# A mixer's head: the order of convolution taps on VectorE, and of halo parts and scalings on GpSimd

## What is computed

```python
x = x + attn_a(layernorm(x))
x = x + ffn(layernorm(x))
x = x + attn_b(layernorm(x))      # the mixer: the change is here
x = x + ffn(layernorm(x))
```

```python
zxbcdt = x @ in_proj_w.T
z, xBC, dt = split(zxbcdt)                       # 512, 640 (x 512, B 64, C 64), 4 columns
dt = softplus(dt + dt_bias)
xBC = silu(causal_depthwise_conv(xBC, conv_w, width=4) + conv_b)
xs, B, C = split(xBC)                            # xs: 4 heads of 128
A = -exp(A_log)
y = ssd(xs * dt, A * dt, B, C) + xs * D          # chunked scan with a state per head
g = y * silu(z)
g = g * rsqrt(mean(g * g) + 1e-5) * norm_w
return g @ out_proj_w.T
```

## Time and profile before

| | us |
|---|---|
| median of 3 runs (546.05, 546.32, 546.50) | 546.32 |
| the profiled execution | 543.31 |
| its span, first to last instruction | 541.5 |
| busy in the span: PE / DVE / ACT / POOL | 517.0 / 402.6 / 310.8 / 127.1 |
| mixer's head, 329.5 to 363.0 | 33.5 |
| chunk loop and projections of the mixer, from 363.0 to about 418 | 55 |

### The profile page before, as it was taken

How to read it: one execution, slowest core, us unless ns; L and a number is a source line. 1 busy time by engine, 2 the same in 40 slices (tenths; PEclk the granted TensorE clock), 3 DMA queues, 4 the chain that set the end, 5 groups by cost and what they waited for, 6 DMA issues and landing times. The chain is left out here.

```text
span 541.5 us, 9132 instructions
## 1 busy us (share of the span) xinstructions
PE 517.0 (95%) x3035; PEld 436.8 (81%) x3037; DVE 402.6 (74%) x899; ACT 310.8 (57%) x768; POOL 127.1 (23%) x272
## 2 busy tenths in 40 slices
PE   5999999999999989999999999999898999999996
PEld 4778899998998977788887888757777778888885
DVE  5625565566566898799987899966886877898767
ACT  3656878588687643573443455889662254443342
POOL 2232424244243310000000004569533100000000
PEclk9999999999999999999999999999999999999999
DMA  7320100000002204000040000000000000000101
GB/s 273 116 79 1 40 2 2 2 0 2 2 2 70 83 1 142 1 1 1 0 137 0 2 1 0 2 0 2 0 1 2 0 1 1 1 1 0 40 1 39
DMA packets 5790, 14.25 MB, mean 26 GB/s; under 512 B 624, under 2 KB 2928, under 8 KB 5744
## 3 DMA queue, kind: packets, MB, share of 16 engines
q1 hardware_dynamic: 5744, 13.66, 7.3%
HBM read 12.61 MB, written 1.05 MB: 25 GB/s over the span
## 5 line engine op out<-in xcount | busy, mean ns | idle before, releaser
L170 PE MATMUL psum<-xT_hl,ffn_w_hl 128*128 128x512 f32 x312 | 77.7, 395 | 0.6 <-DVE f_t L1243 0.4
L170 PE MATMUL psum<-f_um,ffn_w_hl 128*128 128x512 f32 x288 | 72.2, 398 | 1.3 <-DVE f_t L1243 1.3
L170 PEld LDWEIGHTS psum<-xT_hl,ffn_w_hl 128*128 128x128 f32 x312 | 56.2, 188 | 12.2 <-issue 0.9
L170 PEld LDWEIGHTS psum<-f_um,ffn_w_hl 128*128 128x128 f32 x288 | 53.3, 188 | 14.2 <-DVE f_um L1255 2.1
L1140 ACT ACTIVATE f_sil<-psum 128x512 f32<-128x512 f32 (+1 forms) x48 | 28.6, 596 | 60.3 <-PE psum L170 60.0
L170 PE MATMUL psum<-wo_hl,oT_hl 128*128 128x256 f32 x384 | 50.8, 281 | 4.2 <-DVE oT_hl L705 2.6
L699 DVE TENSOR_TENSOR pT_hl<-psum,pT_hl 126x360 fp32r<-126x360 f32 (+1 forms) x44 | 23.6, 537 | 41.4 <-ACT pT_hl L606 41.4
L170 PEld LDWEIGHTS psum<-wo_hl,oT_hl 128*128 128x128 f32 x384 | 47.9, 188 | 7.1 <-DVE oT_hl L705 5.1
L170 PE MATMUL psum<-xT_hl,wq_hl 128*128 128x512 f32 x192 | 52.1, 407 | 0.6 <-ACT qT L572 0.6
L1243 DVE TENSOR_TENSOR f_t<-psum,f_sil 128x512 f32<-128x512 f32 (+1 forms) x48 | 33.2, 691 | 26.2 <-ACT f_sil L1140 25.4
L572 ACT ACTIVATE qT<-psum 128x512 f32<-128x512 f32 x32 | 35.0, 1094 | 29.0 <-PE psum L170 29.0
(11 more groups left out here) (242 smaller groups left out, 1121.4 us busy)
## 6 DMA issues: line engine op xcount, KB each, us to landing
w_raw<-in_wq SPq DMA_DIRECT2D x4, 512.0 KB, 3.3
w_raw<-in_wo SPq DMA_DIRECT2D x4, 512.0 KB, 3.3
ffn_w_raw<-in_ffn SPq DMA_DIRECT2D x3, 576.0 KB, 5.6
ffn_w_raw_far<-in_ffn SPq DMA_DIRECT2D x3, 576.0 KB, 5.2
ssd_w_raw<-in_ssd SPq DMA_DIRECT2D x3, 512.0 KB, 5.7
x_resid<-in_x SPq DMA_DIRECT2D x2, 512.0 KB, 4.4
out_x<-x_resid SPq DMA_DIRECT2D x4, 256.0 KB, 2.2
w_raw<-in_wk SPq DMA_DIRECT2D x1, 512.0 KB, 6.3
```

Of the source, the lines that this page charges most:

```text
L170: i = e.matmul(dst, lhs(a), rhs(b), start=start and n == 0, stop=stop and n == len(TERMS) - 1, **kw)
```

## The change

Nothing that is computed changes; the same 30 taps, 5 joins, silus and scalings are done, in another order.

- Taps: the order is written out as `CV_ORDER`, a list of (i, tap), and with few exceptions neighbouring instructions belong to different tiles. The small instructions of the layer norm, of dt and of the cumulative sum stand at other places between them; ahead of the cumulative sum are now 20 taps, before 18.
- Halo parts: GpSimd works them out for block 0 at once when its tile is there, and for the four heads together, in five instructions with a broadcast of the tap weights, when the last of them (i = 4) is there. Ten instructions in place of 25.
- GpSimd: after make_xd(1) come join(2), join(3), join(4), and behind them make_xd(2) and make_xd(3).
- ScalarE: last_tap(15) moves ahead from behind silu_z(18) to behind silu(3); silu(5) and silu(6) move between the last silu_z's. DA's exponential moves behind the first two exponentials of the loop.
- TensorE: a wait for tile i = 4's taps stands ahead of the cumulative sum's matmuls, since the bank is shared and that tile's last tap is now behind the reciprocal of the dt chain; the keep_busy batches are 4, 7 and 6 long, not 9, 8, 8 and 6.

```diff
-            CONV_RUNS = ((0,), (1,), (2, 3), (4,), (5,), (6, 7), (8, 9))
+            CV_ORDER = [(0, 1), (0, 2), (0, 3), (1, 1), (1, 2), (1, 3), (2, 1), (3, 1), (2, 2), (3, 2), (2, 3), (3, 3),
+                        (4, 1), (4, 2), (5, 1), (4, 3), (5, 2), (6, 1), (5, 3), (6, 2), (7, 1), (6, 3), (7, 2), (8, 1),
+                        (7, 3), (8, 2), (9, 1), (8, 3), (9, 2), (9, 3)]
...
+            def conv_done(e, i):
+
+                e.wait_ge(S["cv"], cv_at(i, TAPS))
...
                 e.wait_ge(S["dt_pool"], DT_DONE)
+                conv_done(e, 4)
                 e.matmul(bank(0)[:, 0:P], a_rep, upto, start=True, stop=True)
...
                     if c == 0:
                         e.wait_ge(S["ipz"], len(others))
-                        keep_busy(9, 6)
-                        e.wait_ge(S["cv"], cv_count(NC))
-                        keep_busy(8, 6)
+                        conv_done(e, NC - 1)
+                        keep_busy(4, 6)
                         e.wait_ge(S["sl"], NC)
-                        keep_busy(8, 6)
+                        keep_busy(7, 6)
                         e.wait_ge(S["L"], 1)
                         keep_busy(6, 6)
...
                 silu_z(16)
                 silu(3)
+                last_tap(15)
                 silu_z(17)
                 silu(4)
+                silu(5)
                 silu_z(18)
-                last_tap(15)
+                silu(6)
                 silu_z(19)
-                for i in range(NC // 2, NC):
+                for i in range(7, NC):
                     silu(i)
-                e.wait_ge(S["cm"], 3)
-                e.activation(DA, DA, ACT.Exp).then_inc(S["da"], 1)
...
                         e.activation(bank(1), bank(1), ACT.Exp).then_inc(S["L"], 1)
+                        if c == 0:
+                            e.wait_ge(S["cm"], 3)
+                            e.activation(DA, DA, ACT.Exp).then_inc(S["da"], 1)
...
-                conv(0)
+                conv((0, 1), (0, 2))
                 ln["norm"](e, 1)
-                conv(1)
+                conv((0, 3), (1, 1), (1, 2))
                 ln["lo"](e, 1)
-                conv(2, 3)
+                conv((1, 3), (2, 1), (3, 1), (2, 2), (3, 2), (2, 3), (3, 3))
...
-                conv(4)
+                conv((4, 1), (4, 2), (5, 1))
                 e.wait_ge(S["dt_pool"], 5)
                 e.reciprocal(R1, N1).then_inc(S["dt_dve"], 1)
-                conv(5)
+                conv((4, 3), (5, 2), (6, 1), (5, 3), (6, 2))
...
-                conv(6, 7)
-                conv(8, 9)
+                conv((7, 1), (6, 3), (7, 2), (8, 1), (7, 3), (8, 2), (9, 1), (8, 3), (9, 2), (9, 3))
...
+                def carries(n, tiles, last):
+
+                    e.wait_ge(S["tap"], last + 1)
+                    b0, nb = tiles.start, tiles.stop - tiles.start
+                    taps = par[:, PR_CW + CONV * b0:PR_CW + CONV * (b0 + nb)].rearrange("p (b k) -> p b k", b=nb)
+                    tap = lambda k, wide: taps[:, :, k:k + 1].broadcast_to([P, nb, wide])
+                    e.tensor_tensor(carry[:, tiles, :], halo[:, tiles, :], tap(0, TAPS), ALU.mult)
+                    e.tensor_tensor(parts[:, tiles, 0:2], halo[:, tiles, 1:3], tap(1, 2), ALU.mult)
+                    e.tensor_tensor(parts[:, tiles, 2:3], halo[:, tiles, 2:3], tap(2, 1), ALU.mult).then_inc(S["part"], 1)
...
+                carries(0, slice(0, 1), 0)
+                carries(1, slice(2, CB), NC // 2 - 1)
...
                 join(1)
-                for i in range(1, NH):
-                    make_xd(i)
-                    join(i + 1)
+                make_xd(1)
+                for i in range(2, NH + 1):
+                    join(i)
+                make_xd(2)
+                make_xd(3)
```

More of the change, by code:

```diff
@@ L1470, in mixer @@
             dst = lambda b: cb_pre[:, :] if b == 0 else xs[:, b - 2, :]
-            names = ("xda dtw dtv cs cm rhs mb sel gs da raw wh wl bcz ip tap ipz part carry join cv sl xd dt dt_dve dt_pool dt_act de L G xt X xdd wt ce Y St st1 st y g ghi glo g2 ss "
+            names = ("xda dtw dtv cs cm rhs mb sel gs da raw wh wl bcz ip tap ipz part join cv sl xd dt dt_dve dt_pool dt_act de L G xt X xdd wt ce Y St st1 st y g ghi glo g2 ss "
                      "ve ri O fin bt").split()
@@ L1489, in mixer @@
             NC = len(convs)
-            CONV_RUNS = ((0,), (1,), (2, 3), (4,), (5,), (6, 7), (8, 9))
+            CV_ORDER = [(0, 1), (0, 2), (0, 3), (1, 1), (1, 2), (1, 3), (2, 1), (3, 1), (2, 2), (3, 2), (2, 3), (3, 3),
+                        (4, 1), (4, 2), (5, 1), (4, 3), (5, 2), (6, 1), (5, 3), (6, 2), (7, 1), (6, 3), (7, 2), (8, 1),
+                        (7, 3), (8, 2), (9, 1), (8, 3), (9, 2), (9, 3)]
+            assert len(CV_ORDER) == TAPS * NC
             def cv_at(i, tap):
[L1495 to L1502, removed]
+                return CV_ORDER.index((i, tap)) + 1
+            def conv_done(e, i):
+                e.wait_ge(S["cv"], cv_at(i, TAPS))
             def bank_taken(e, n):
                 if n in convs:
-                    e.wait_ge(S["cv"], cv_count(convs.index(n) + 1))
+                    conv_done(e, convs.index(n))
                 else:
@@ L1641, in decays @@
                         e.wait_ge(S["cm"], 3)
[L1642 removed]
+                        conv_done(e, 5)
                     else:
@@ L1752, in silu @@
                     b, h = order[convs[i]]
-                    e.wait_ge(S["cv"], cv_count(i + 1))
+                    conv_done(e, i)
                     if h:
@@ L1846, in dve, with conv @@
                 ln["veps"](e, 1)
[L1848 to L1860, removed]
-                conv(0)
+                emitted = iter(CV_ORDER)
+                def conv(*taps):
+                    for i, d in taps:
+                        assert next(emitted) == (i, d)
+                        b, h = order[convs[i]]
+                        src = bank(IN_BANK[convs[i]])
+                        out = dst(b)[:, half(h)]
+                        tap = par[:, PR_CW + CONV * b + CONV - 1 - d:PR_CW + CONV * b + CONV - d]
+                        e.wait_ge(S["tap"], i + 1)
+                        if d > 1:
+                            e.wait_ge(S["cv"], cv_at(i, d - 1))
+                        e.scalar_tensor_tensor(out=out[:, d:HALF], in0=src[:, 0:HALF - d], scalar=tap,
+                                               in1=out[:, d:HALF], op0=ALU.mult, op1=ALU.add).then_inc(S["cv"], 1)
+                conv((0, 1), (0, 2))
                 ln["norm"](e, 1)
-                conv(1)
+                conv((0, 3), (1, 1), (1, 2))
                 ln["lo"](e, 1)
-                conv(2, 3)
+                conv((1, 3), (2, 1), (3, 1), (2, 2), (3, 2), (2, 3), (3, 3))
                 e.wait_ge(S["dt"], 1)
@@ L1984, in join @@
                     out = dst(b)[:, HALF:HALF + TAPS]
-                    e.wait_ge(S["cv"], cv_count(NC // 2 + i + 1))
-                    e.wait_ge(S["carry"], i + 1)
+                    conv_done(e, NC // 2 + i)
+                    e.wait_ge(S["part"], 3 if b == 0 else 6)
                     e.tensor_tensor(out, out, carry[:, b, :], ALU.add).then_inc(S["join"], 1)
```

18 lines of the change are left out of this document (7 added, 11 removed).

## The result

The changed kernel takes 541.55 us (median of 7 runs, 540.86 to 541.93). The kernel before, run beside it, now has a median of 544.15 us over 7 runs: the three of 546.05 to 546.5 that the prediction saw, and four new ones at 543.54 to 544.15. The ratio of the two is 0.9937, with a 95% interval of 0.9916 to 0.9958. The medians are 2.6 us apart, the forecast was 2.5. The profiled execution is at 540.87 us with a span of 539.1; by the same subtraction from the profiled execution of before the prediction had 540.8.

The account below looks back on a forecast made before the run. The head was taken as bound by whichever of VectorE's taps, GpSimd's order and ScalarE's queue releases silu(9) last. Taps 1.3, GpSimd's order 1.1 and DA's exponential 0.14 make 2.5 us: 546.32 becomes 543.8 us, range 542.6 to 546.0.

Parts of the forecast that it names:

- What bounds the head: Mixer's head: the loop's first exponential waits for silu(9), that for join(4), which GpSimd does only after make_xd(3).
- Alternating taps, 0.8 us: VectorE: a dependent neighbouring tap costs 0.20 us; four such neighbours instead of eight save 0.8 us.
- both idle times, 0.54: VectorE: its waits for the cumulative sum, 0.33 us, and for tile 15's first tap, 0.21 us, both go.
- the second wait: VectorE waiting for tile 15's first tap on ScalarE at 355.33 us, put at 0.21 us, to disappear.
- GpSimd's order, 1.1 us: GpSimd: with joins ahead of make_xd(2) and (3), join(4) waits only for the last tap; 1.1 us gained.
- ScalarE's queue: ScalarE must be through with silu(8) by 358.5 us; expected free at 358.5, with 359.6 as upper bound.
- DA's exponential, 0.14: ScalarE: moving this exponential from ahead of the loop to behind its first two exponentials gains 0.14 us.
- Halo parts, select(1), x_dt_decay under cover: GpSimd: halo work for tiles 1 to 4 and later select(1) cost nothing; x_dt_decay keeps 0.85 us of cover.
- The price of a fall there, 5.2 us: TensorE ahead of the loop: its clock falls, two chunks at half rate cost 5.2 us, giving 549.0; chance 0.06.
- Sum, 2.5 us: Whole head: 1.3 from taps, 1.1 from GpSimd's order and 0.14 from DA's exponential make 2.5 us; chance 0.67.
- 543.31 becomes 540.8; the median becomes 543.8: Whole kernel: 2.5 us taken off the profiled execution and off the three runs' median of 546.32 us.
- The rivals: Gaps not from dependence 0.05, alternation fails 0.05, no change 0.07, TensorE's clock falls 0.06, partial gain 0.10.

Follow-up runs that it names:

- a_taps_in_runs: The changed kernel with the taps in the old order (tiles 0, 1, 4, 5 alone, the others in pairs); median 543.66 us.
- best_order: The changed kernel with three more dependent neighbours taken apart in the tap order; median 540.76 us, ratio to the kernel before 0.9937.
- a_joins_between: The changed kernel with GpSimd's old order, make_xd and join alternating; median 544.68 us.
- a_busy_0: The changed kernel without any of the 17 keep_busy matmuls ahead of the loop, the waits kept; median 544.63 us.

## Why the prediction was right in its mechanism and wrong in its time

- **What bounds the head: right.** silu(9) was released by join(4), join(4) by make_xd(3). With the joins ahead, join(4) and silu(9) behind it wait for the last tap.
- **Alternating taps, 0.8 us, and both idle times, 0.54: right.** 1.3 foretold; from the first tap the last one ends 26.02 - 24.53 = 1.49 us earlier. The forecast counted 0.8 + 0.54 = 1.34. Of the 0.15 beyond that, 0.09 is the second wait, which cost 0.30 us and not the 0.21 that its row shows (a_taps_in_runs); 0.06 I can't name. best_order confirms the price of 0.20 for one more dependence. From the Trainium skill's "VectorE: DVE Perf Modes", section "The DRAIN you can't avoid", the prediction drew that a tap behind its own predecessor steps like any other; that is not borne out for these shapes, 0.86 against 0.655 in both records. The same section also says that an instruction that is not held starts earlier, which agrees with independent taps of 0.74 us that start 0.655 apart.
- **GpSimd's order, 1.1 us: right,** 1.04 by itself. The three terms do add in the whole change, 1.49 + 1.04 + 0.14 = 2.67. They don't when one is missing, since silu(9) starts with the last queue to arrive: without this order the rest is worth 0.53 (a_joins_between).
- **ScalarE's queue: right.** It was through with silu(8) at 358.31 (358.5 foretold), 0.27 us ahead of join(4).
- **DA's exponential, 0.14: right.**
- **Halo parts, select(1), x_dt_decay under cover: right,** x_dt_decay kept 1.02 us (0.85 foretold).
- **TensorE.** The gap was 1.29 us, 1.0 foretold; the clock held at 1.00. Not said: the shorter batches are needed for 1.07 us of the gain. The price of a fall there, 5.2 us, was three times too high: a_busy_0 paid 1.67 for it.
- **Sum, 2.5 us: right,** 2.67 at decays(1), 2.65 between the kernels with the filled gap, 2.6 between the medians.
- **"543.31 becomes 540.8; the median becomes 543.8": this is the step that failed.** The first half was measured at 540.87. The second half took the median of three runs for a property of the kernel. I had written that it lay 3.0 us above the profiled execution and did not ask why: a change of head can't be told from a level that an execution has by chance. All three runs lay where before's slowest lie, 545.5 to 546.5. The record of such an execution shows a slow start of 1.3 us and a fall of the clock behind the gap ahead of project(7) of 1.5 us, together more than the whole change. That those three runs had the lower clock is inferred from their times, since they have no record; two later executions at 546.1 do show it.
- **The rivals.** None took place: the alternation works, the loop does start on silu(9), the clock holds at 357 to 372 us. The fall that I had looked for in the head sat 55 us later, in the kernel before as well.

## What to carry to other kernels

When several queues meet at one instruction, it starts with the last of them, and an edit shows its worth only once the others are out of the way: two parts of this change worth 1.04 and 0.53 us alone gave 2.55 together, and matmuls without use that were counted for the old wait took back 1.07 of it when kept. Where a profiled execution and the timed runs stand further apart than the change is worth, find out first what the difference is, by the granted clock beside each run, and forecast a difference or work from the execution that you have read. A gap of 1 us on TensorE can cost more than it lasts, here 1.5 us in the record that shows the fall; with four matmuls without use in it none of 24 runs had the lower clock.

## What the runs showed of the hardware that was not expected

- Two VectorE instructions of 128 x 511 elements start 0.655 us apart if they are independent, 0.86 if the second waits for the first, whatever stands two places back.
- Five operations on GpSimd with tap weights broadcast over 12 elements or fewer take 0.21 us each, one on 3 elements with a scalar operand 0.31.
- Behind an idle gap of TensorE of only 1.03 us, followed by eight matmuls of one column, one core's granted clock fell to the lower level (0.53 over 3.6 us in one record). 35 of 88 executions of the kernel before have the mean clock, 0.997 or 0.996, that goes with it; in the others the same gap left the clock alone. It did not fall behind the 1.29 us ahead of the loop in the record of after, nor when the gap was cut to 0.17 us (0 of 12, 0 of 6 and 0 of 6 runs). An idle time of 5.48 us dropped it to 0.50 in the record and cost 1.67 us up to project(7).
- The twelve matmuls of L415 at 9.4 us take 3.31 us in one execution and 4.43 in another of the same kernel, and everything behind lies 1.3 us later, with the column of the granted clock at 1.00 in both.
